# Attention with routed experts: the layer norm's small steps on GpSimd, a paced end of the scatters, and the second bf16 parts on ScalarE

## What is computed

```
xn  = layernorm(x)                                   # over 256
out = x + attention(xn) + experts(xn)

attention: Q, K, V = relu(xn @ W + b), 16 heads of 16
           scores = Q K^T / 4; masked where a row sum of xn is 0, and causally
           a = softmax(scores) V + xn;  gamma * layernorm(a) + beta
experts:   logits = xn @ router_w.T + bias; the best 2 of 8, softmax over the two
           sum of w_e * (silu(xn w1_e) * (xn w3_e)) w2_e, and one shared expert
```

## Time and profile before

| what | value |
|---|---|
| median of 3 | 2209.66 us (2207.64 to 2210.34) |
| the profiled execution | 2199.74 us, span 2198.0 us |
| attention phase in it | to about 1157 us |
| mean granted TensorE clock | 0.952 |

### The profile page before, as it was taken

The page is one execution under the profiler, slowest core; times in us unless marked ns, Lnnn a source line. Parts: engine busy times, 40 slices in busy tenths (PEclk is TensorE's granted clock), DMA queues, the critical chain, the costliest instruction groups (busy, mean ns, idle before and its releaser), DMA issues. The chain is left out here.

```text
span 2198.0 us, 37336 instructions
## 1 busy us (share of the span) xinstructions
PE 1900.2 (86%) x13238; PEld 1375.1 (63%) x13238; DVE 1401.7 (64%) x2935; ACT 1082.8 (49%) x2048; POOL 1129.4 (51%) x935
## 2 busy tenths in 40 slices
PE   0368988888888888899676999999999999899998
PEld 0245544454554444555325888888888888788887
DVE  6577887788878888876513465656565543355556
ACT  0115555555455555555344666666666665333232
POOL 5444324544554454453423676867777764344443
PEclk9769999999999999999878999999999999999999
DMA  1653655666566666666345566666666654334443
GB/s 36 115 98 81 115 100 120 131 123 129 124 128 136 122 128 125 123 124 129 96 145 168 178 208 203 211 204 199 211 194 216 191 182 153 115 118 141 142 141 110
DMA packets 235391, 314.01 MB, mean 143 GB/s; under 512 B 18986, under 2 KB 200372, under 8 KB 229044
## 3 DMA queue, kind: packets, MB, share of 16 engines
q1 hardware_dynamic: 222964, 278.63, 51.0%
q0 software_dynamic: 12288, 33.57, 4.8%
HBM read 211.43 MB, written 100.70 MB: 142 GB/s over the span
## 5 line engine op out<-in xcount | busy, mean ns | idle before, releaser
L495 ACT ACTIVATE pT<-st_ps 128x512 f32<-128x512 f32 (+1 forms) x704 | 384.1, 559 | 477.0 <-PE st_ps L995 382.1
L1671 PE MATMUL gu<-xc,w_up_h 128*128 128x512 f32 x1760 | 553.1, 396 | 23.6 <-POOL w_up_l L1370 17.1
L719 DVE TENSOR_REDUCE mx<-s_ps 128x1 f32<-128x512 f32 (+3 forms) x704 | 436.2, 638 | 154.3 <-PE s_ps L974 123.4
L972 PE MATMUL s_ps<-k_aug,q_aug 97*128 97x512 bf16 (+3 forms) x1024 | 294.5, 320 | 138.8 <-DVE mx L719 124.0
L1671 PEld LDWEIGHTS gu<-xc,w_up_h 128*128 128x128 f32 x1760 | 326.3, 190 | 103.9 <-issue 18.0
L1671 PE MATMUL gu<-xc,w_up_l 128*128 128x512 f32 x880 | 345.1, 392 | 0.0
L1548 DVE TENSOR_TENSOR hf<-sil,gu 128x512 f32<-128x512 f32 x220 | 151.0, 686 | 258.8 <-ACT sil L1467 258.6
L1370 POOL TENSOR_TENSOR w_up_l<-w_raw,w_up_h 128x512 fp32r<-128x512 f32 x160 | 204.0, 1298 | 210.9 <-ACT w_up_h L1462 210.9
L993 PE MATMUL st_ps<-q_aug,k_aug 99*128 99x512 bf16 (+3 forms) x1024 | 286.5, 313 | 21.8 <-ACT pT L495 14.2
L972 PEld LDWEIGHTS s_ps<-k_aug,q_aug 97*128 97x128 bf16 x1024 | 101.9, 101 | 321.5 <-DVE mx L719 233.3
L411 POOL DMA_INDIRECT expert_rows<-xrow,slot x128 | 125.2, 978 | 314.5 <-DMA q_aug<-neg_scr 249.2
(11 more groups left out here) (207 smaller groups left out, 3418.1 us busy)
## 6 DMA issues: line engine op xcount, KB each, us to landing
w_raw<-in_L_ffn_w_dram SPq DMA_DIRECT2D x117, 512.0 KB, 6.0
part_scr<-parts SPq DMA_DIRECT2D x64, 384.0 KB, 9.3
q_aug<-part_scr SPq DMA_DIRECT2D x192, 128.0 KB
k_aug<-part_scr SPq DMA_DIRECT2D x192, 128.0 KB
xr<-expert_rows SPq DMA_DIRECT2D x39, 512.0 KB
expert_results<-yo SPq DMA_DIRECT2D x39, 512.0 KB, 3.3
x_sb<-in_L_attn_x_dram SPq DMA_DIRECT2D x16, 512.0 KB
layernorm_rows<-xn SPq DMA_DIRECT2D x16, 512.0 KB
```

Source lines behind the costliest of these rows:

```text
L495: fn(pT[:, j % 2, h:h + heads, 0:w], unit_view(st_ps[u % 2], heads, w), ACT.Exp).then_inc(exp_done, 1)
L719: vec.tensor_reduce(mx[:, q, h:h + heads], unit_view(s_ps[u % 2], heads, keys), AX_X, ALU.max).then_inc(s_max, 2)
L972: mm(v[:, n], q_aug[par][0:ROWS_S, h0 + n, P * q:P * (q + 1)], k_aug[par][0:ROWS_S, h0 + n, 0:keys], start=True, stop=False)
L1671: last = mm(gu[m % 2][:, a], w_up[wpar][x][:, a, c, P * m:P * (m + 1)], xc[par][:, y, c], start=k == 0, stop=k == 3 * NC - 1)
```

## The change

- VectorE keeps the reductions and the wide operations of the norm, now partly in halves of two tiles (ln_mean, ln_var, ln_masks), the three reciprocals and the two bit masks. [...] Each hand-over is a semaphore: mean_part, mean_ready, var_part, s1_ready, r0_ready, d1_ready, r1_ready, root_ready, rd_ready, mask_part, mask_sum. The units of the steps move by one to three.
- second_part goes from VectorE to ScalarE, at units 12, 14, 19 and 22.
- The last scatters: batches 11, 12 and 13 in iteration 14, and 14 and 15 in iteration 15, each pair of DMAs behind a wait for the exponentials of units 2, 5, 8 and so on. SP fetches the batches earlier and writes the ends of four experts in iteration 14 and of the other four in 15, no longer behind a wait for all scatters; that wait stands at the end of SP's program.

```diff
-        AT_SECOND = (11, 13, 17, 23)
+        AT_SECOND = (12, 14, 19, 22)
-        AT_NORM = (1, 2, 3, 14, 15, 18, 20, 24, 26, 41, 42)
+        AT_MEAN, AT_CENTRE, AT_VAR = (1, 2), 4, (13, 14)
+        AT_R0, AT_R1, AT_RD, AT_QUOT, AT_BITS = 18, 20, 23, 25, 27
+        AT_MASKS = (40, 41, 43)
...
         def scattered_in(i):
-            if i == B - 1:
-                return list(range(B - GB, B))
-            return [i - 3] if 3 <= i < B - 1 else []
+            if i >= B - 2:
+                return {B - 2: [B - 5, B - 4, B - 3], B - 1: [B - 2, B - 1]}.get(i, [])
+            return [i - 3] if i >= 3 else []
...
+                for b in scattered_in(i)[2:]:
+                    fetch(b)
+                if i == B - 2:
+                    fill_ends(range(E // 2))
                 if maxima:
                     load_neg(i + 1, 1 - par, 0)
                 for b in scattered_in(i + 1)[:2]:
                     fetch(b)
-                for b in scattered_in(i)[2:]:
-                    fetch(b)
                 if i == B - 1:
-                    fill_ends()
+                    fill_ends(range(E // 2, E))
...
+            small_begin, small_mark, small_op, small_end = chain(pool, chain_small, 28)
+            def fold4(a, b, final):
+                small_op(gp.tensor_tensor(tree2[:], a, b, ALU.add))
+                t2 = tree2[:].rearrange("p t (a b) -> p t a b", b=2)
+                small_op(gp.tensor_tensor(tree3[:], t2[:, :, :, 0], t2[:, :, :, 1], ALU.add))
+                return gp.tensor_tensor(final, tree3[:, :, 0], tree3[:, :, 1], ALU.add)
...
+            def small_mean(b):
+                small_begin(b)
+                await_(pool, mean_part, 2 * (b + 1))
+                small_op(fold16(s[SUM]))
+                await_(pool, a_ready, b)
+                gp.tensor_tensor(s[MEAN], s[SUM], inverse, ALU.mult).then_inc(mean_ready, 1)
+            def small_variance(b):
+                await_(pool, var_part, 2 * (b + 1))
+                small_op(fold4(lanes[:, :, 0:4], lanes[:, :, 4:8], s[SUM]))
+                small_op(gp.tensor_tensor(s[T1], s[SUM], inverse, ALU.mult))
+                small_op(gp.tensor_tensor(s[V1], s[T1], eps, ALU.add))
+                gp.tensor_tensor(s[S0], s[V1], half[:], ALU.pow).then_inc(s1_ready, 1)
+            def small_step(b):
+                await_(pool, r0_ready, b + 1)
+                small_op(gp.tensor_tensor(s[Q1], s[V1], s[R0], ALU.mult))
+                small_op(gp.tensor_tensor(s[T1], s[Q1], s[S0], ALU.add))
+                gp.tensor_tensor(s[D1], s[T1], half[:], ALU.mult).then_inc(d1_ready, 1)
+            def small_root(b):
+                await_(pool, r1_ready, b + 1)
+                small_mark(gp.tensor_tensor(s[SL], s[D1], s[SH], ALU.subtract))
...
+                gp.tensor_tensor(s[ROOT], s[T1], s[D1], ALU.add).then_inc(root_ready, 1)
+            def small_parts(b):
+                await_(pool, root_ready, b + 1)
+                await_(pool, rd_ready, b + 1)
+                small_mark(gp.tensor_tensor(s[DL], s[ROOT], s[DH], ALU.subtract))
+                small_op(gp.tensor_tensor(s[NRD], s[RD], minus, ALU.mult))
+            def small_mask(b):
+                await_(pool, mask_part, 2 * (b + 1))
+                await_(pool, mk_ready, b)
+                fold16(s[MASK_SUM]).then_inc(mask_sum, 1)
...
-                for b in mine if one is None else []:
-                    scatter(b, range(NT))
+                if norm:
+                    small_mean(i + 3)
+                if one is None:
+                    for n in range(len(mine) * NT):
+                        await_(pool, exp_done, NU * i + 2 + 3 * n)
+                        scatter(mine[n // NT], [n % NT])
...
                 if norm:
-                    await_(pool, v1_ready, i + 4)
-                    gp.tensor_tensor(sm[:, 2], sm[:, 1], half[:], ALU.pow).then_inc(s1_ready, 1)
+                    small_variance(i + 3)
                 if project:
                     second(i + 2, 2)
+                if norm:
+                    small_step(i + 3)
                 if project:
                     second(i + 2, 3)
                     third(i + 2, 2)
+                if norm:
+                    small_root(i + 3)
                 if one is not None:
                     scatter(one, [2])
                 if project:
                     third(i + 2, 3)
                 if norm:
+                    small_parts(i + 3)
                     quotient(i + 3)
                 if one is not None:
                     scatter(one, [3])
+                if norm:
+                    small_mask(i + 3)
...
+            def second_part(b, k):
+                await_(act, r1_done, 2 * NC * b + k + 1)
+                u = TILE_ORDER[k]
+                fn(parts[:, 1, u], r1[:, u], ACT.Copy).then_inc(b1_done, 1)
...
+            def ln_mean(b, h):
+                if h == 0:
+                    await_(dve, x_in, 16 * (b + 1))
+                    await_(dve, mask_sum, b)
+                row_sums(x_sb, h).then_inc(mean_part, 1)
             def ln_centre(b):
-                ln(vec.tensor_scalar(sm[:, MEAN], sm[:, SUM], 1.0 / C, None, ALU.mult))
+                await_(dve, mean_ready, b + 1)
+                await_(dve, normed, b)
...
+            def ln_r1(b):
+                await_(dve, d1_ready, b + 1)
+                vec.reciprocal(s[R1], s[D1])
+                vec.tensor_scalar(s[SH].bitcast(U32), s[D1].bitcast(U32), HIGH_BITS, None, ALU.bitwise_and
+                                  ).then_inc(r1_ready, 1)
+            def ln_rd(b):
+                await_(dve, root_ready, b + 1)
...
+                await_(dve, mask_sum, b + 1)
+                mask(vec.tensor_scalar(msk[:], s[MASK_SUM], 0.0, None, ALU.not_equal))
```

More of the change, by code:

```diff
@@ L106, in attention_phase @@
         cmask = sb("cmask", [P, 2, P], BF16)
-        half = sb("half", [P, NT])
+        half, norm_consts = sb("half", [P, NT]), sb("norm_consts", [P, 3, NT])
         zeros = sb("zeros", [P, NT, C])
@@ L289, in fetch, with fill_ends @@
                 sp.dma_start(xrow[:, b % 2], xn_dram[b].rearrange("(t p) c -> p t c", p=P)).then_inc(row_in[b % 2], 16)
-            def fill_ends():
+            def fill_ends(experts):
                 await_(sp, table_ready, 1)
-                for k in range(2):
-                    await_(sp, scattered[k], 16 * 2 * NT * (B // 2))
-                for e in range(E):
+                for e in experts:
                     sp.reg_load(end_reg, carry_i[0:1, e:e + 1])
@@ L366, in body @@
                     fetch(b)
-                for b in scattered_in(i)[2:]:
-                    fetch(b)
                 if i == B - 1:
-                    fill_ends()
+                    fill_ends(range(E // 2, E))
             iterations(sp, body)
+            for k in range(2):
+                await_(sp, scattered[k], 16 * 2 * NT * (B // 2))
             await_(sp, filled, 16 * E)
@@ L383, in _ @@
             gp.memset(one[:], 1.0).then_inc(consts, 1)
-            await_(pool, consts, 4)
+            for k, value in enumerate((1.0 / C, LN1_EPS, -1.0)):
+                gp.memset(norm_consts[:, k], value).then_inc(consts, 1)
+            await_(pool, consts, 7)
             gp.affine_select(out=identf[:], in_=identf[:], compare_op=ALU.is_equal, fill=0.0, base=0,
@@ L424, in third @@
                 gp.tensor_tensor(parts[:, 2, u], r1[:, u], parts[:, 1, u], ALU.subtract).then_inc(b2_done, 1)
+            s = [sm[:, k] for k in range(20)]
+            inverse, eps, minus = (norm_consts[:, k] for k in range(3))
+            small_begin, small_mark, small_op, small_end = chain(pool, chain_small, 28)
[4 more added lines that the diff above has]
+                return gp.tensor_tensor(final, tree3[:, :, 0], tree3[:, :, 1], ALU.add)
@@ L540, in body @@
                         tile_out(i + 2, AT_K.index(s))
+                    if s in AT_SECOND and project:
+                        second_part(i + 2, AT_SECOND.index(s))
                     if s == AT_COPY[0] and attend:
@@ L647, in _ @@
-            s = [sm[:, k] for k in range(20)]
-            def ln_root(b):
-                await_(dve, s1_ready, b + 1)
-                ln(vec.reciprocal(s[R0], s[S0]))
-                ln(vec.tensor_tensor(s[Q1], s[V1], s[R0], ALU.mult))
-                ln(vec.tensor_tensor(s[T1], s[Q1], s[S0], ALU.add))
-                ln(vec.tensor_scalar(s[D1], s[T1], 0.5, None, ALU.mult))
-                ln_mark(vec.reciprocal(s[R1], s[D1]))
-                ln(vec.tensor_scalar(s[SH].bitcast(U32), s[D1].bitcast(U32), HIGH_BITS, None, ALU.bitwise_and))
@@ new lines, in ln_r0 @@
+            def ln_r0(b):
+                await_(dve, s1_ready, b + 1)
+                vec.reciprocal(s[R0], s[S0]).then_inc(r0_ready, 1)
+            def ln_r1(b):
[5 more added lines that the diff above has]
+                await_(dve, root_ready, b + 1)
+                vec.reciprocal(s[RD], s[ROOT])
```

(8 more changed lines are left out.)

147 lines of the change are left out of this document (68 added, 79 removed).

## The result

| kernel | median us | runs |
|---|---|---|
| before, same chip | 2210.0 | 4 |
| changed | 2114.1 (2113.6 to 2116.8) | 4 |

The ratio is 0.9571, 95% interval 0.9554 to 0.9587: 96 us faster. 2142 was forecast, with a range of 2112 to 2188. The profiled execution of the changed kernel took 2113.83 us for a span of 2112.1.

A forecast was written before the change was run, and what follows sets the result against it. TensorE, busy 86% of the span, was taken as the bound, kept waiting in full iterations by VectorE-only work. 52 (full iterations) + 20 (tail) - 4 (prologue) = 68 us less, 2142 us, range 2112 to 2188.

The forecast's parts named there:

- Full iterations: Iterations 0 to 12: small steps to GpSimd and casts to ScalarE save 4.0 us each, 52 us, ends 20 and 66.
- the walk: Iteration at 725.80 followed step by step in the new order: quotient 2 us earlier, VectorE waiting at units 4, 23, 40, 43.
- the most is 5.1 us per iteration: Upper limit of the gain per full iteration, taken from iteration 13, which has no layer norm and takes 57.00 us.
- The deductions of 0.4 and 0.7: Taken off 5.1 us per iteration: 0.4 for ScalarE's casts, 0.7 for VectorE's waits at units 4, 23, 40 and 43.
- Tail: Iterations 14 and 15: redistributed last scatters save 20 of ScalarE's 33.4 us of remote waits, bounds 5 and 33.
- it regulates itself: Last scatters: each pair waits for exponentials, so it can't run ahead of stalled engines; ground for the 20 us.
- part 3: End of the scatters: 24 in iteration 14 and 16 in 15, in pairs, end fills split; 20 us less.
- Prologue: Before batch 0, where nothing hides the chain: small steps and hand-overs on GpSimd cost 4 us, bounds 2 and 9.
- Slower, small steps dear: Rival: GpSimd's small steps take 0.70 us instead of 0.28, each of 13 iterations 4.1 us longer, 2247 us; chance 0.09.
- The hand-overs eat the gain: Rival: ScalarE waits for remainders and VectorE for GpSimd, 1.5 us gain per iteration remains, 2174 us; chance 0.14.
- The tail does not move: Rival: any dense scatter brings the delay, 24 in one iteration as bad as 8 and 16, 2162 us; chance 0.16.
- both parts at their best: Rival: full iterations gain 66 us and the tail 33, less 4 for the prologue, 95 in all, 2115 us; chance 0.03.

The follow-up runs named there:

- the kernel of parts 1 and 2: Kernel before with the norm's small steps on GpSimd and casts on ScalarE, old scatter end: 2103.5 us, ratio 0.9690; on another chip 2106.3 us, ratio 0.9703.
- the steps put back on VectorE: Changed kernel with 29 extra 128x4 steps per normalised batch on VectorE that nothing reads: 2166.4 us, ratio 0.9838 to the kernel before.
- part 2 alone: Kernel before with only the four casts moved to ScalarE, at units 12, 14, 19 and 22: 2133.1 us against 2171.9, ratio 0.9817.
- part 1 without part 2: Kernel before with only the norm's small steps moved to GpSimd, casts still on VectorE: 2157.0 us, ratio 0.9940.
- the unpaced kernel: Changed kernel with the scatters of iterations 14 and 15 issued back to back, without waiting for exponentials: 2094.1 us, ratio 0.9648 to the kernel before.
- 11 more steps: Changed kernel with 11 more 128x4 steps on GpSimd, between tile 2's third part and the scatter: 2172.9 us, ratio 0.9863 to the kernel before.

## Why the prediction was right, and where its terms were off

**Full iterations: 52 forecast, 62.9 measured (4.0 and 4.84 each).** The mechanism is shown from both sides: the waits went where the walk had put them, and putting VectorE's time or GpSimd's time back brings iterations of 62.1 and 62.0 us on average (63.0 before, 58.1 changed). The term that was mis-sized is "the most is 5.1 us per iteration". It starts from the one iteration at 725.80, 62.10 us, but the thirteen take 62.98 on average: iterations 2, 6 and 10 take 64.9, 67.5 and 65.5. The changed kernel's take 58.14, which is 1.14 over iteration 13's 57.00, and 0.4 and 0.7 had been taken off for that. So the end was as forecast, "57 to 59 us", and the start was 0.88 us too low: 13 x 0.88 = 11.4 us, the whole miss of 10.9. The same iteration of the changed kernel, at 679.00, is 4.2 us shorter than the one at 725.80, near the 4.0.

Iteration 13 was no true floor either, though the sum did not fail by it: its granted clock was 0.94, and with the clock at 1.00 the kernel of parts 1 and 2 took 54.8 us for it.

**What the clock is worth.** TensorE's busy time fell by 24.3 us, and the sum has no term for it. But busy time is not time of the iteration. Iteration 5 of the kernel before, on two chips:

```profile
471.90:533.90 62.00, 52.87 (x465) 30.23 (x465) 50.26 (x125) 33.55 (x63) 30.82 (x23) 1.00 0.66 129
```
```profile
476.00:538.10 62.10, 56.65 (x465) 32.22 (x465) 50.33 (x125) 33.85 (x64) 30.82 (x23) 0.92 0.67 130
```

In both TensorE pauses 2.2 us at the same place for the maxima. In the first the clock does not fall, in the second it does, at the iteration's start and again behind that pause; TensorE is busy 3.8 us longer, and the iteration takes the same 62.07 us from exponential to exponential. TensorE's speed is not what sets the time there; the lower clock only fills its idle time. In the changed kernel it can be otherwise. The first 12 units of iteration 2, again on two chips:

```profile
270.30:288.90 18.60, 16.18 (x133) 8.72 (x131) 14.99 (x35) 12.41 (x23) 2.38 (x7) 1.00 0.79 116
```
```profile
269.00:290.50 21.50, 19.08 (x133) 10.20 (x131) 14.98 (x35) 12.40 (x23) 2.38 (x7) 0.84 0.71 112
```

The pauses of TensorE are the same, and all 2.9 us of busy time that the lower clock adds are added to the stretch. How much of the 62.9 us is due to the clock is not shown; it is not simply 24.3. In iterations 5, 7 and 8, which the kernel before ran at 1.00, the change gained 3.9, 3.9 and 5.1 us without any help of the clock.

**The deductions of 0.4 and 0.7** stood for real waits (ScalarE 3.0 us before remainders, VectorE 0.5 at unit 4, 1.7 at unit 18, 0.5 at 20 and 0.6 at 23, of which the walk had not foreseen those at 18 and 20, and none at the first masks' sum, which begins at 732.23, the moment the quotient's last operation ends). How much of the 4.84 they cost can be bounded: the steps put back on VectorE give 806.8 us with all hand-overs in place, part 2 alone 789.2 with the same steps on VectorE and none of part 1's hand-overs; 17.6 us over 13 iterations, 1.4 each, if all of it is theirs (the two ran on different chips). The two deductions together, 1.1, agree with the 1.14 above; how it splits between them is not shown.

**Part 1 against part 2.** The prediction added them up. They don't add: 38.8 and 14.9 us alone, 68.4 together. The 3.1 us in which VectorE waits for remainders were priced with part 2, rightly; what was not said is that part 1 without part 2 would have enlarged them.

**Tail: 20 forecast, 21.7 measured.** ScalarE's remote waits, in the changed kernel from 960 to 1074 (compare):

```profile
ACT pT L579 <- remote: 6.0, 2, 3.7
```

Under 15 us, as said (the row has 33.4); iteration 14 is at 56.5 us ("near 57"). The size is right and its grounds only in part. Against the chip without stalls (50.3 and 32.5 us) the kernel before lost 19.8 and 15.4 us in the two iterations, the changed one 6.2 and 9.3: 19.7 us less. VectorE had remote waits too, 15.9 us before its maxima in the kernel before and 0.9 in the changed one. But that "it regulates itself" by the pacing is argued, not shown: the unpaced kernel was equal where nothing stalls, and it was not run where something does. And the old place of the waits for the scatters, which "cover nothing either", cost nothing only where the stall outlasts the fills; on a chip without it their place is worth 10 us, the whole gain of part 3 there.

**Prologue: 4 slower forecast, 0.7 faster measured.** The first transposes come at 60.22 us, 2.7 later:

```profile
60.22 1.09 PE L1008 MATMUL misc<-identf,xn 128*128 128x128 f32 x4 [34.87 <-DVE mk L770]
```

That half is as said, with hand-overs a little cheaper (61.5 was written). The step that failed is "in the next two iterations the gains and losses offset each other": they gain 3.4 us. With 11 more steps the transposes come at 63.27, 3.05 us later still, 0.28 a step.

**The rivals.** *Slower, small steps dear:* the steps took 0.28 us, and the 0.61 row stood for nothing here. But the break-even that I gave, 0.57 us a step, was too generous. 11 steps of 0.28 more are what 0.43 us in each of the 21 would be, and they already took 63 of the 96 us. The wait was foreseen ("2.5 to 3 us more"), the clock behind it and the start of the kernel were not. *The hand-overs eat the gain:* fell with the iterations of 57 to 58 us; one unit off in the casts' place, though, and it comes nearly true (43 us lost). *The tail does not move:* fell on the first chip; on the one where both kernels were traced again the tail's mechanism is another.

**The rule on offloading** between VectorE and GpSimd was outweighed, but it is not empty. The 128x4 steps on GpSimd kept their 0.20 us beside VectorE's maxima, and the first fold's 1.04 us left VectorE with its steps; so did one of 0.62 us on average (line 653) that the sum priced at 0.20. In their place another small operation of VectorE is long, the bits at unit 20, 0.92 us on average where its like three units later takes 0.20. Groups of VectorE's instructions by line, 230 to 915:

```profile
L734 DVE TENSOR_SCALAR sm<-sm 128x4 uint32<-128x4 uint32 x12 | 11.0, 918 | 0.0
...
L740 DVE TENSOR_SCALAR sm<-sm 128x4 uint32<-128x4 uint32 x12 | 2.4, 199 | 0.0
```

The one at 709.10 takes 1.00 us and ends at 710.10, with GpSimd's remainder of 1.16 us that began at 708.92. A second one, the bf16 rounding of the negative maxima (line 797), takes 0.50 us at 710.73, beside GpSimd's third part of 710.03, and 0.18 at 736.01. Two stretched operations per iteration, some 1.1 us, are the price, not 32.

**A slip in the count.** The prediction has four wide operations split in halves for three more instructions; three are split (ln_mean, ln_var, ln_masks), and the three more are right.

The range of 2112 to 2188 held the time, near its lower end, where "both parts at their best" (2115) had been put at 0.03. Of the 28 us between 2142 and 2114 the full iterations make 10.9, the start of the kernel 4.7, the tail 1.7 and iteration 13 0.6. The other 10 come from carrying the distance between profile and median of the kernel before over to the changed one, which shows none (2113.8 and 2114.1).

## What to carry to other kernels

Price a change from the mean of the iterations, not from one that looks typical: 0.88 us in one was the whole miss over thirteen. Read a stretch that is taken as a floor with its clock: below 1.00 it is no floor. TensorE's busy time lost to a low clock is time lost only where TensorE has no slack; compare the same iteration with and without the fall before pricing it. A wait of ScalarE or VectorE matters by what is queued behind it. Work moved to the idle engine pays only if its place in that engine's order leaves the hand-over behind what the other engine reaches by itself; a unit or two too early cost some 43 us here, 3.1 us of chain some 63.

## What the runs showed of the chip that I had not expected

- The tail's stall belongs to the chip as much as to the kernel: 33.4 us of ScalarE's remote waits on the chip of the profile, none on a second with the same kernel, and none on a third with the same scatters. Where the tail stalls, there is one such wait in the second half too, 11.2 to 11.4 us of ScalarE in all six traces, far from these scatters, and in none of the others. A wait called remote should be looked for on a second chip before it is priced.
- The lower clock follows a pause and outlasts it: 0.50 while TensorE is busy 2.00 us of 2, for about 3.4 us behind the pause of 3.3 us. It does not follow every pause: the same one of 2.2 us in iteration 5 of the kernel before had it on one chip and not on the other, at no difference in time.
- 3.1 us more per iteration on an engine busy 37 us in 58 took two thirds of the gain of the whole change.
